# A graph kernel whose final normalization moves from VectorE to ScalarE, with another plan for its banks

## The chip, the core and the metric

The kernel runs on one core of a Trainium2 chip. The metric is the time of one execution on the device, in microseconds (us). The engines of the core are named as in the profile: PE is TensorE (PEld its weight loads), DVE is VectorE, ACT is ScalarE, POOL is GpSimd, SP is SyncE, which here only starts transfers. TensorE writes its results to eight banks of PSUM, each of 128 partitions by 512 fp32 values.

## The reference

128 graphs of 64 nodes with 256 features pass through two layers, each with a residual and a normalization without learned factors. The first layer is attention with 8 heads and a mask for each head, the second a graph network with 4 heads and a gate:

```python
def _layernorm(x, axis=-1, eps=1e-05):
    m = jnp.mean(x, axis=axis, keepdims=True)
    v = jnp.var(x, axis=axis, keepdims=True)
    return (x - m) / jnp.sqrt(v + eps)

def layer0(x, masks):                       # q, k, v: x @ W.T + b, split in 8 heads
    scores = where(mask, q @ k.T / sqrt(32), -1e9)
    return softmax(scores) @ v, merged, @ Wo.T + bo

def layer1(h, adj):                         # 4 heads
    Wh = h @ W.T + bW
    A = tanh(where(adj, (Wh @ attn) @ Wh.T, 0))
    ha = concat(relu(A @ Wh)) @ A_w.T
    hf = h @ fc_w.T
    coeff = sigmoid(hf @ g1_w.T + ha @ g2_w.T + gbias)
    return hf * coeff + ha * (1 - coeff)

h   = _layernorm(x + layer0(x, masks))
out = _layernorm(h + layer1(h, adj))
```

The change touches the last line: how the mean, the variance and the quotient of the second normalization are worked out for each group, and where its input lies meanwhile.

## The kernel before

Eight graphs (512 nodes) form a group; there are 16 groups, 0 to 15. The kernel is written as one program for each engine, in a fixed order, and the engines meet at semaphores. All engines walk through 17 **turns**. A turn has an A group and a B group: it does the first layer of group A and the second layer of group B = A - 1, with the instructions of the two interleaved. `whole(eng, turn)` writes them out: turn 0 (A = 0, no B), turn 1 (1, 0), a hardware loop over turns 2 to 14, turn 15 (A = 15, B = 14), and the last turn (no A, B = 15).

Precise products are made of three fp32r matmuls, so most tensors exist as a high part that ScalarE copies out of a bank (`T_out`, `U_high`, `cat_high`, ...) and a low part that VectorE forms from the same bank (`low`).

**Banks.** Each result of TensorE has a name (T0 to T7, score0 to score3, R0, ...) and a bank. The strings `BODY`, `FIRST` and `LAST` near the top list all results of a turn in TensorE's order as `name:bank`. Before TensorE writes a result, `claim` makes it wait until the result that had this bank before has been released: each bank has a semaphore `taken` that its last reader raises (`take`), and one named `full` that TensorE raises (`filled`) and readers wait for (`await_tile`). A bank is thus a ring: what follows what in it comes from the list alone.

**The end of a group.** Behind the gate, VectorE leaves the transposed sum `rT`. TensorE transposes it back (`res_T`) into the banks R0 and R1, two of the group's four blocks p of 256 features in each, as the last thing of turn g + 1 for B = g. ScalarE copies both to `res` in SBUF (`res_out`, 128x512 each), at the end of the same turn, and in the last turn behind T3 for group 14. At the start of the next turn VectorE takes the moments of `res` (`result_moments`: four BN_STATS, four BN_AGGR, giving mean and variance `mv2`), GpSimd adds EPS and takes the power -0.5 (`root_2`, giving `rstd2`), and VectorE normalizes `res` in place, block by block (`result_normalized`), between its first score tile (`shift(A, 0)`) and its second. SP then stores `res` (`store`, 512 KB). For group 15, functions with `half` in their names do this in the last turn, with VectorE reading the banks; they are the same before and after.

**The start of a turn.** TensorE computes T0, then the scores of A, then T1 to T7, hf0 and the adj products (`adj_scores`, which wait for T4 to T7 to be released). ScalarE copies each T tile out and runs an exponential of the softmax (`exps`) behind T1, T3, T5 and T7, as `EXP_AFTER` says. The softmax of a score tile on VectorE is `shift` (add the mask, take the maximum, subtract it: lines L1112, L1115, L1117), on ScalarE the exponential (L861), on VectorE the sum and its reciprocal, on GpSimd the product of both (L1386).

In the profile's rows a bank is just `bank`. The lines that matter: L389, L390 and L394 are the three matmuls of `dense` (all T tiles among others), L516 the scores, L602 adj, L709 the R transposes; L885 `T_out`, L861 `exps`, L949 `res_out`, L875 at_hi of `attention`, L848 the queries' copy; L1176 and L1180 the moments, L1272 `result_normalized`; L1403 and L1405 `root_2`, L1396 a small product of `root_1`; L699 the last turn's transposes, L1243 its rT.

Of the kernel before, what the change touches and what calls it, by code (L numbers as in the profile page):

```python
# [10 lines left out]
ALU = mybir.AluOpType  # L11
# [26 lines left out]
def listed(text):  # L38
# [9 lines left out]
BODY = ("T0:4 score0:0 score1:1 score2:2 score3:3 T1:5 T2:6 T3:7 T4:4 T5:5 T6:6 T7:7 hf0:4 adj0:5 adj1:6 v0:0 v1:1 "  # L48
        "probT0:2 probT1:3 probT2:0 probT3:1 U000:7 U001:4 U010:5 U011:6 U100:2 U101:3 U110:0 U111:1 attn0:7 attn1:4 "
        "hf1:5 cat0:6 cat1:2 cat2:3 cat3:7 y0:0 y1:1 cat4:4 cat5:5 cat6:6 cat7:7 ha0:4 ha1:5 z0:6 z1:7 hT0:2 hT1:3 ")  # L50
# [8 lines left out]
def stage_kernel(nc, x, xT, adjS, adjT, masks, eye, wq, bq, wk, bk, wv, bv, wo, bo,  # L59
                 Wn, attn, AwT, fcn, g1T, g2T, gb, out):  # L60
    ctx = ExitStack()
    with ctx:
# [21 lines left out]
        def sb(name, shape, dt=F32):  # L84
            return at(name, shape, dt, region(size(shape, dt)))
# [57 lines left out]
        rstd1, rstd2, var1, from1 = (sb(n, [P, NP]) for n in ("rstd1", "rstd2", "var1", "from1"))  # L143
# [55 lines left out]
        zeros_ready = sem("zeros_ready")  # L199

# [87 lines left out]
        def _(sp):  # L288
# [65 lines left out]
            def store(g):  # L354
                sp.wait_ge(out_ready, g * NP + NP)
                carried(sp)
                sp.dma_start(out[bass.ds(g, 1)].rearrange("o p t d -> t (o p) d"), res[:]).then_inc(stored, 16)
# [13 lines left out]
            for s in range(2):  # L371

                sp.wait_ge(out_ready, (GROUPS - 1) * NP + 2 * s + 2)
                sp.dma_start(out[GROUPS - 1, 2 * s:2 * s + 2].rearrange("p t d -> t p d"),
                             res[:, 2 * s:2 * s + 2, :]).then_inc(stored, 16)
# [404 lines left out]
        def _(act):  # L780
# [162 lines left out]
            def res_out(g):  # L943
                if later(g):
                    act.wait_ge(stored, g * 16)
                    carried(act)
                for q2 in range(2):
                    bank = await_tile(act, "B", f"R{q2}", g)
                    take(act.activation(res[:, 2 * q2:2 * q2 + 2, :], pairs_of(bank), ACT.Copy), "B", f"R{q2}", g)  # L949

            def turn(A, B, more):
# [39 lines left out]
                for n in range(KC):  # L991
                    T_out(B, n)
                    if A is None and n == 3:
                        res_out(B - 1)
                    if A is not None and n in EXP_AFTER:
                        exps(A, EXP_AFTER.index(n))
                h_fc(B, 0)
# [26 lines left out]
                if more:  # L1024
                    queries(A + 1)
                    keys(A + 1)
                    res_out(B)
# [4 lines left out]
        def _(dve):  # L1032
# [231 lines left out]
            def result_moments(g):  # L1264
                for q2 in range(2):
                    await_taken(dve, "B", f"R{q2}", g)
                moments(g, res, stats2, mv2, stats2_ready, mv2_ready)

            def result_normalized(g):
                dve.wait_ge(rstd2_ready, g + 1)  # L1270
                for p in range(NP):
                    dve.tensor_scalar(res[:, p, :], res[:, p, :], mv2[:, p, 0:1], rstd2[:, p:p + 1], ALU.subtract,  # L1272
                                      ALU.mult).then_inc(out_ready, 1)

            def turn(A, B, more):
# [27 lines left out]
                if later(B):  # L1303
                    result_normalized(B - 1)
# [36 lines left out]
        def _(pool):  # L1341
# [58 lines left out]
            def root_2(g):  # L1400
                pool.wait_ge(mv2_ready, g * NP + NP)
                carried(pool)
                pool.tensor_scalar(rstd2[:], mv2[:, :, 1], EPS, None, ALU.add).then_inc(root2, 1)  # L1403
                pool.wait_ge(root2, g + 1)
                pool.tensor_tensor(rstd2[:], rstd2[:], half[:], ALU.pow).then_inc(rstd2_ready, 1)  # L1405

# [94 lines left out]
```

## Time and profile before

| | |
|---|---|
| median of 3 runs | 1094.99 us (1093.66 to 1097.73) |
| the profiled execution | 1096.53 us, of which the span from first to last instruction is 1094.4 us |
| mean granted clock of TensorE | 0.998 |
| busy: PE, PEld, DVE, ACT, POOL | 1079.4, 905.4, 732.6, 531.4, 284.1 us |
| instructions | 25365 |
| chain of work that ended last | PE 97%, DVE 2%, DMA 1% |

Busy time of an engine is the time in which at least one of its instructions runs. Matmuls are pipelined, and their ends in the trace are modelled, so the start of one and the start of the next say more than its length. In the rows, "idle before" in brackets is the time for which the engine had stood idle and what ended it; a row without brackets followed the one before it at once. A row with x4 stands for four instructions in a row, with their time together.

### The profile page before, as it was taken

Reading aid. Unit: us, or ns where it says so; the run is one execution under the profiler, and the core shown is the slowest. Engines: PE = TensorE matmul, PEld = TensorE weight load, DVE = VectorE, ACT = ScalarE, POOL = GpSimd, SP = SyncE. Lnnn points to the kernel's source line nnn. Section 1 sums busy time; section 2 is a strip of 40 time slices with the busy share of each in tenths; the row PEclk is TensorE's granted clock in tenths of the full one; section 3 lists DMA queues with packets and bytes.
Section 4 is the critical chain, followed back from the end, with each engine's and each line's share of the span. In section 5 each row is a group of like instructions: output and inputs, shape, how many; then the busy total and the mean of one; then the engine's idle time right before and its main releaser. Section 6 shows DMA issues by size and latency. Waiting matters only on the chain.

```text
span 1094.4 us, 25365 instructions
## 1 busy us (share of the span) xinstructions
PE 1079.4 (99%) x10090; PEld 905.4 (83%) x10090; DVE 732.6 (67%) x1379; ACT 531.4 (49%) x947; POOL 284.1 (26%) x249
## 2 busy tenths in 40 slices
PE   8999999999999999999999999999999999999997
PEld 6888788888888888788888888888888888888886
DVE  7785766767677585765757667585775757667545
ACT  5663453635446363563635446363563635536351
POOL 1542231231322213222231312213222232312200
PEclk9999999999999999999999999999999999999999
DMA  7000100100010000100100010000100001010000
GB/s 263 2 25 19 41 24 27 34 20 19 22 40 22 20 19 22 40 22 20 41 19 21 22 40 22 20 19 22 40 22 20 31 13 37 22 41 3 1 20 20
DMA packets 26860, 32.59 MB, mean 30 GB/s; under 512 B 4432, under 2 KB 23376, under 8 KB 26448
## 3 DMA queue, kind: packets, MB, share of 16 engines
q1 hardware_dynamic: 26400, 31.93, 8.7%
q8 instruction: 21, 0.34, 0.1%
q10 hardware_dynamic: 432, 0.26, 0.1%
q14 instruction: 7, 0.06, 0.0%
HBM read 23.80 MB, written 8.39 MB: 29 GB/s over the span
## 4 chain that ended last, share of the span: by engine, by line
PE 97%; DVE 2%; DMA 1%; issue 0%; POOL 0%; ACT 0%; DVEq 0%
PE bank L389 18%; PE bank L390 17%; PE bank L394 17%; PE bank L381 8%; PE bank L383 8%; PE bank L382 8%; PE bank L602 5%; PE bank L625 4%; PE bank L529 2%; PE bank L516 2%; PE bank L547 2%; PE bank L572 1%; PE bank L709 1%; PE bank L429 0%; DMA raw_q<-in_wq 0%
## 5 line engine op out<-in xcount | busy, mean ns | idle before, releaser
L920 ACT ACTIVATE cat_hi<-bank 128x512 fp32r<-128x512 f32 x128 | 76.6, 598 | 128.5 <-PE bank L394 128.5
L885 ACT ACTIVATE T<-bank 128x512 f32<-128x512 f32 x128 | 75.8, 594 | 78.4 <-PE bank L394 78.1
L1034 DVE SCALAR_TENSOR_TENSOR cat_lo<-bank,cat_hi 128x512 fp32r<-128x512 f32 x128 | 86.5, 685 | 40.6 <-ACT cat_hi L920 39.7
L389 PE MATMUL bank<-hT_hi,g_lo 128*128 128x512 f32 x256 | 102.7, 401 | 0.0
L383 PE MATMUL bank<-cat_hi,aw_hi 128*128 128x512 f32 (+1 forms) x272 | 102.4, 377 | 0.0
L382 PE MATMUL bank<-cat_hi,aw_lo 128*128 128x512 f32 (+1 forms) x272 | 102.4, 377 | 0.0
L381 PE MATMUL bank<-cat_lo,aw_hi 128*128 128x512 f32 (+1 forms) x272 | 102.4, 377 | 0.0
L1386 POOL TENSOR_TENSOR probs<-probs,den 128x512 f32<-128x512 f32 x64 | 67.1, 1059 | 131.5 <-DVE den L1125 131.5
L390 PE MATMUL bank<-hT_hi,g_hi 128*128 128x512 f32 x256 | 99.9, 390 | 0.0
L390 PE MATMUL bank<-U_hi,wt_hi 128*128 128x512 f32 x256 | 99.8, 390 | 0.0
L389 PE MATMUL bank<-U_hi,wt_lo 128*128 128x512 f32 x256 | 99.8, 390 | 0.0
L1034 DVE SCALAR_TENSOR_TENSOR haT_lo<-bank,haT_hi 128x512 fp32r<-128x512 f32 (+1 forms) x34 | 22.4, 660 | 113.1 <-ACT haT_hi L925 106.1
L1034 DVE SCALAR_TENSOR_TENSOR U_lo<-bank,U_hi 128x512 fp32r<-128x512 f32 x128 | 78.0, 681 | 12.9 <-ACT U_hi L914 12.9
L1379 POOL TENSOR_TENSOR y<-y,bo_all 128x1024 f32<-128x1024 f32 x16 | 39.1, 2441 | 176.6 <-ACT at_hi L875 176.6
L925 ACT ACTIVATE haT_hi<-bank 128x512 fp32r<-128x512 f32 x30 | 17.9, 598 | 125.8 <-PE bank L383 125.8
L394 PE MATMUL bank<-hT_lo,g_hi 128*128 128x512 f32 x256 | 78.9, 389 | 0.0
L394 PE MATMUL bank<-U_lo,wt_hi 128*128 128x512 f32 x256 | 78.9, 389 | 0.0
L914 ACT ACTIVATE U_hi<-bank 128x512 fp32r<-128x512 f32 x128 | 64.4, 626 | 7.3 <-PE bank L625 7.3
L1369 POOL TENSOR_TENSOR hT<-hT_hi,hT_lo 128x1024 f32<-128x1024 f32 x16 | 38.8, 2422 | 107.7 <-DVE hT_lo L1034 107.7
L861 ACT ACTIVATE probs<-probs 128x512 f32<-128x512 f32 x64 | 40.4, 632 | 38.5 <-DVE probs L1117 38.4
L382 PEld LDWEIGHTS bank<-cat_hi,aw_lo 128*128 128x128 f32 x272 | 51.2, 188 | 9.4
L381 PEld LDWEIGHTS bank<-cat_lo,aw_hi 128*128 128x128 f32 x272 | 51.2, 188 | 9.4
(183 smaller groups left out, 2768.9 us busy)
## 6 DMA issues: line engine op xcount, KB each, us to landing
y<-in_x SPq DMA_DIRECT2D x16, 512.0 KB, 3.4
out<-res SPq DMA_DIRECT2D x15, 512.0 KB, 3.0
x_raw<-in_xT SPq DMA_DIRECT2D x14, 512.0 KB, 3.3
W_nat<-in_Wn SPq DMA_DIRECT2D x1, 1028.0 KB, 7.7
attn_nat<-in_attn SPq DMA_DIRECT2D x1, 1024.0 KB, 9.9
adjS_u<-in_adjS SPq DMA_DIRECT2D x32, 32.0 KB, 2.7
raw_A<-in_AwT SPq DMA_DIRECT2D x1, 1024.0 KB, 8.7
x_second<-in_xT SPq DMA_DIRECT2D x1, 512.0 KB, 10.1
```

What stands on the lines that cost most here:

```text
L381: pe.matmul(out, asel(a[0]), bsel(b[1]), start=first, stop=False)
L382: pe.matmul(out, asel(a[1]), bsel(b[0]), start=False, stop=False)
L383: return pe.matmul(out, asel(a[0]), bsel(b[0]), start=False, stop=last)
L389: pe.matmul(out, wsel(w[1]), dsel(d[0]), start=first and n == 0, stop=False)
L390: pe.matmul(out, wsel(w[0]), dsel(d[0]), start=False, stop=False)
L394: ins = pe.matmul(out, wsel(w[0]), dsel(d[1]), start=False, stop=last and n == len(terms) - 1)
L602: ins = pe.matmul(bank[b * S:b * S + S, q * D:q * D + D].rearrange("p (h n) -> p h n", h=H2), hT[:, k, first:first + S], T[:, k, :, first: ...
L885: take(act.activation(T[:, n % DC, n // DC, :], bank[:], ACT.Copy), "B", f"T{n}", g)
L914: act.activation(U_hi[:, c, :, first:first + P], bank[:].rearrange("p (h t) -> p h t", h=H2), ACT.Copy).then_inc(U_hi_ready, 1)
L920: act.activation(cat_hi[:, n, :], bank[:], ACT.Relu).then_inc(cat_hi_ready, 1)
L1034: return dve.scalar_tensor_tensor(out=out, in0=bank, scalar=bias, in1=hi.bitcast(F32), op0=op, op1=ALU.subtract)
L1386: pool.tensor_tensor(view, view, den[:, j, :].unsqueeze(2).to_broadcast([P, NG, S]), ALU.mult) \
```

## The change

The change has three parts. First, `res_out` no longer copies: ScalarE writes the normalized result straight from the banks, four activations of 128x256 with the scale `rstd2` and the bias `from2` = -mean x rstd2, one pair for each block. It has moved from the end of the turn to the place behind T1 and the first exponential of the next turn (in the last turn from behind T3 to behind T5), and waits for `from2`. VectorE takes the moments from the banks, and `result_normalized` is gone. Second, GpSimd makes `from2` in two further small instructions. Third, since R0 and R1 now stay in banks 6 and 7 until after T1, `BODY` gives T0 to T3 the banks 4, 5, 4, 5, and banks 4 and 6, and 5 and 7, are exchanged for all results behind. SP's store waits for R0 and R1 to be released instead of for `out_ready`. The `LAST` list is as it was.

```diff
-BODY = ("T0:4 score0:0 score1:1 score2:2 score3:3 T1:5 T2:6 T3:7 T4:4 T5:5 T6:6 T7:7 hf0:4 adj0:5 adj1:6 v0:0 v1:1 "
+BODY = ("T0:4 score0:0 score1:1 score2:2 score3:3 T1:5 T2:4 T3:5 T4:6 T5:7 T6:4 T7:5 hf0:6 adj0:7 adj1:4 v0:0 v1:1 "
...
             def store(g):
-                sp.wait_ge(out_ready, g * NP + NP)
-                carried(sp)
+                for q2 in range(2):
+                    await_taken(sp, "B", f"R{q2}", g)
+                    carried(sp)
                 sp.dma_start(out[bass.ds(g, 1)].rearrange("o p t d -> t (o p) d"), res[:]).then_inc(stored, 16)
...
             def res_out(g):
+
                 if later(g):
                     act.wait_ge(stored, g * 16)
                     carried(act)
-                for q2 in range(2):
-                    bank = await_tile(act, "B", f"R{q2}", g)
-                    take(act.activation(res[:, 2 * q2:2 * q2 + 2, :], pairs_of(bank), ACT.Copy), "B", f"R{q2}", g)
+                act.wait_ge(from2_ready, g + 1)
+                carried(act)
+                for p in range(NP):
+                    bank = bank_of("B", f"R{p // 2}", g)
+                    ins = act.activation(res[:, p, :], bank[:, p % 2 * D:p % 2 * D + D], ACT.Identity,
+                                         bias=from2[:, p:p + 1], scale=rstd2[:, p:p + 1])
+                    if p % 2:
+                        take(ins, "B", f"R{p // 2}", g)
...
                 for n in range(KC):
                     T_out(B, n)
-                    if A is None and n == 3:
-                        res_out(B - 1)
                     if A is not None and n in EXP_AFTER:
                         exps(A, EXP_AFTER.index(n))
+                    if (n == 5 if A is None else n == 1) and later(B):
+                        res_out(B - 1)
...
                 if more:
                     queries(A + 1)
                     keys(A + 1)
-                    res_out(B)
...
             def result_moments(g):
-                for q2 in range(2):
-                    await_taken(dve, "B", f"R{q2}", g)
-                moments(g, res, stats2, mv2, stats2_ready, mv2_ready)
-
-            def result_normalized(g):
-                dve.wait_ge(rstd2_ready, g + 1)
                 for p in range(NP):
-                    dve.tensor_scalar(res[:, p, :], res[:, p, :], mv2[:, p, 0:1], rstd2[:, p:p + 1], ALU.subtract,
-                                      ALU.mult).then_inc(out_ready, 1)
+                    if p % 2 == 0:
+                        bank = await_tile(dve, "B", f"R{p // 2}", g)
+                    dve.bn_stats(stats2[:, p, :], bank[:, p % 2 * D:p % 2 * D + D]).then_inc(stats2_ready, 1)
+                dve.wait_ge(stats2_ready, g * NP + NP)
+                carried(dve)
+                for p in range(NP):
+                    dve.bn_aggr(mv2[:, p, :], stats2[:, p, :]).then_inc(mv2_ready, 1)
...
                 if A is not None:
                     shift(A, 0)
-                if later(B):
-                    result_normalized(B - 1)
...
                 pool.tensor_tensor(rstd2[:], rstd2[:], half[:], ALU.pow).then_inc(rstd2_ready, 1)
+                pool.tensor_scalar(from2[:], mv2[:, :, 0], -1.0, None, ALU.mult).then_inc(neg2, 1)
+                pool.wait_ge(rstd2_ready, g + 1)
+                pool.wait_ge(neg2, g + 1)
+                carried(pool)
+                pool.tensor_tensor(from2[:], from2[:], rstd2[:], ALU.mult).then_inc(from2_ready, 1)
```

The next rows are ScalarE's order at the start of the looped turn, before the change, with what each instruction waits for (`full4` is bank 4 filled, `shifted` a score tile shifted):

```order
L885 ACTIVATE T<-bank 128x512 [waits full4]
L244 REGISTER_ALU
L885 ACTIVATE T<-bank 128x512 [waits full5]
L860 ISA
L861 ACTIVATE probs<-probs 128x512 [waits shifted]
L244 ISA
L885 ACTIVATE T<-bank 128x512 [waits full6]
```

And after it:

```order
L887 ACTIVATE T<-bank 128x512 [waits full4]
L245 REGISTER_ALU
L887 ACTIVATE T<-bank 128x512 [waits full5]
L862 ISA
L863 ACTIVATE probs<-probs 128x512 [waits shifted]
L948 ISA
L954 ACTIVATE res<-bank,from_118,rstd_115 128x256 [waits stored,from2_ready]
L954 ACTIVATE res<-bank,from_118,rstd_115 128x256 x3
L887 ACTIVATE T<-bank 128x512 [waits full4]
```

Four res activations stand between the first exponential and T2, and T2 comes out of bank 4 instead of 6.

TensorE's order before, from the first matmul of T3 to that of T4 (each T tile is six matmuls; the claim of its bank is the wait in front of the first, and L236 only computes what count to wait for):

```order
L389 MATMUL bank<-hT_hi,g_lo 128x512 [waits taken7]
L390 MATMUL bank<-hT_hi,g_hi 128x512
L389 MATMUL bank<-hT_hi,g_lo 128x512
L390 MATMUL bank<-hT_hi,g_hi 128x512
L394 MATMUL bank<-hT_lo,g_hi 128x512 x2
L389 MATMUL bank<-hT_hi,g_lo 128x512 [waits taken4]
```

And after it, the same place:

```order
L391 MATMUL bank<-hT_hi,g_lo 128x512 [waits taken5]
L392 MATMUL bank<-hT_hi,g_hi 128x512
L391 MATMUL bank<-hT_hi,g_lo 128x512
L392 MATMUL bank<-hT_hi,g_hi 128x512
L396 MATMUL bank<-hT_lo,g_hi 128x512 x2
L237 ISA
L391 MATMUL bank<-hT_hi,g_lo 128x512 [waits taken6]
```

The matmuls are the same. T3 now waits for T1's bank, and T4 for bank 6, which R0 had.

## Rows read from the trace of the kernel before

**Rows 1.** the profile's page: the span, then busy time of TensorE (PE)

```profile
span 1094.4 us, 25365 instructions
...
PE 1079.4 (99%) x10090; PEld 905.4 (83%) x10090; DVE 732.6 (67%) x1379; ACT 531.4 (49%) x947; POOL 284.1 (26%) x249
```

**Rows 2.** TensorE's waits, first and last of seven: us in total, times, longest

```profile
PE bank L516 <- issue: 1.8, 2, 1.1
PE bank L699 <- DVE rT L1243: 1.7, 2, 1.4
...
PE bank L475 <- DVE x_lo L1053: 0.2, 1, 0.2
```

**Rows 3.** busy time by stretch (instructions), then granted clock, DMA share, GB/s

```profile
117.00:121.00 4.00, 2.89 (x134) 2.26 (x133) 2.40 (x9) 0.60 (x1) 1.27 (x2) 1.00 0.02 4
512.07:527.11 15.04, 15.04 (x193) 12.28 (x193) 12.46 (x28) 8.06 (x14) 3.35 (x4) 1.00 0.10 35
```

**Rows 4.** TensorE's weight loads (PEld) that begin T3, T4, T5 and T6

```profile
518.57 0.19 PEld L389 LDWEIGHTS bank<-hT_hi,g_lo 128*128 128x128 f32 x1
...
519.93 0.19 PEld L389 LDWEIGHTS bank<-hT_hi,g_lo 128*128 128x128 f32 x1
...
521.29 0.19 PEld L389 LDWEIGHTS bank<-hT_hi,g_lo 128*128 128x128 f32 x1
...
522.65 0.19 PEld L389 LDWEIGHTS bank<-hT_hi,g_lo 128*128 128x128 f32 x1
```

**Rows 5.** ScalarE (ACT) in time order: start us, us, what, idle before

```profile
512.85 1.08 ACT L949 ACTIVATE res<-bank 128x512 f32<-128x512 f32 x2
...
517.62 0.60 ACT L885 ACTIVATE T<-bank 128x512 f32<-128x512 f32 x1 [2.51 <-PE bank L394]
518.16 0.63 ACT L861 ACTIVATE probs<-probs 128x512 f32<-128x512 f32 x1
518.99 0.60 ACT L885 ACTIVATE T<-bank 128x512 f32<-128x512 f32 x1 [0.20 <-PE bank L394]
...
521.50 0.63 ACT L861 ACTIVATE probs<-probs 128x512 f32<-128x512 f32 x1 [0.56 <-DVE probs L1117]
522.04 0.58 ACT L885 ACTIVATE T<-bank 128x512 f32<-128x512 f32 x1
...
540.31 1.63 ACT L875 ACTIVATE at_hi<-bank,bias_v 128x256 fp32r<-128x256 f32 x4
```

**Rows 6.** VectorE (DVE) in time order, the same turn

```profile
514.03 1.41 DVE L1176 BATCH_NORM_STATS2 stats<-res 128x6 f32<-128x256 f32 x4 [3.20 <-ACT res L949]
515.60 0.38 DVE L1180 BATCH_NORM_AGGREGATE mv<-stats 128x2 f32<-128x6 f32 x4 [0.16 <-DVE stats L1176]
515.99 0.69 DVE L1112 TENSOR_TENSOR probs<-bank,mask_static 128x512 f32<-128x512 f32 x1
...
517.43 0.69 DVE L1117 TENSOR_TENSOR probs<-probs,mx 128x512 f32<-128x512 f32 x1
518.04 1.38 DVE L1272 TENSOR_SCALAR res<-res,mv,rstd 128x256 f32<-128x256 f32 x4
```

**Rows 7.** GpSimd (POOL) in time order, the same turn

```profile
488.50 0.20 POOL L1396 TENSOR_TENSOR var<-var,rstd 128x4 f32<-128x4 f32 x1
...
516.17 0.23 POOL L1403 TENSOR_SCALAR rstd<-mv 128x4 f32<-128x4 f32 x1 [7.95 <-DVE mv L1180]
516.48 1.04 POOL L1405 TENSOR_TENSOR rstd<-rstd,half 128x4 f32<-128x4 f32 x1
```

**Rows 8.** ScalarE by line: duration ns min/median/max, first and last start

```profile
L848 ACT ACTIVATE qT<-bank,bias_q x32: 687/690/695, 8.5 to 971.1; 128x512 f32<-128x512 f32 x32
...
L875 ACT ACTIVATE at_hi<-bank,bias_v x64: 467/551/568, 32.6 to 1003.8; 128x256 fp32r<-128x256 f32 x64
```

**Rows 9.** ScalarE and TensorE late in the T tiles of the last turn

```profile
1044.36 0.60 ACT L885 ACTIVATE T<-bank 128x512 f32<-128x512 f32 x1 [0.76 <-PE bank L394]
...
1048.33 0.63 PEld L602 LDWEIGHTS bank<-T,hT 128*64 128x64 f32 x8 [0.35 <-issue]
```

More of the change, by code:

```diff
@@ L47 @@
                "G7:2 W0:5 W1:6 W2:7 W3:1 q0:4 q1:2 FC:5 FF:6 hT0:0 hT1:3 k0:7 k1:1")
-BODY = ("T0:4 score0:0 score1:1 score2:2 score3:3 T1:5 T2:6 T3:7 T4:4 T5:5 T6:6 T7:7 hf0:4 adj0:5 adj1:6 v0:0 v1:1 "
-        "probT0:2 probT1:3 probT2:0 probT3:1 U000:7 U001:4 U010:5 U011:6 U100:2 U101:3 U110:0 U111:1 attn0:7 attn1:4 "
-        "hf1:5 cat0:6 cat1:2 cat2:3 cat3:7 y0:0 y1:1 cat4:4 cat5:5 cat6:6 cat7:7 ha0:4 ha1:5 z0:6 z1:7 hT0:2 hT1:3 ")
+BODY = ("T0:4 score0:0 score1:1 score2:2 score3:3 T1:5 T2:4 T3:5 T4:6 T5:7 T6:4 T7:5 hf0:6 adj0:7 adj1:4 v0:0 v1:1 "
+        "probT0:2 probT1:3 probT2:0 probT3:1 U000:5 U001:6 U010:7 U011:4 U100:2 U101:3 U110:0 U111:1 attn0:5 attn1:6 "
+        "hf1:7 cat0:4 cat1:2 cat2:3 cat3:5 y0:0 y1:1 cat4:6 cat5:7 cat6:4 cat7:5 ha0:6 ha1:7 z0:4 z1:5 hT0:2 hT1:3 ")
 TURN = listed(BODY + "q0:0 q1:1 k0:2 k1:3 R0:6 R1:7")
@@ L142, in stage_kernel @@
         mv1, mv2 = (sb(n, [P, NP, 2]) for n in ("mv1", "mv2"))
-        rstd1, rstd2, var1, from1 = (sb(n, [P, NP]) for n in ("rstd1", "rstd2", "var1", "from1"))
+        rstd1, rstd2, var1, from1, from2 = (sb(n, [P, NP]) for n in ("rstd1", "rstd2", "var1", "from1", "from2"))
         W_nat = at("W_nat", [P, DC * H2, D + 1], F32, r_cat)
@@ L199, in stage_kernel @@
         zeros_ready = sem("zeros_ready")
+        neg2, from2_ready = sem("neg2"), sem("from2_ready")
         def carried(eng):
@@ L371, in _ @@
             for s in range(2):
-                sp.wait_ge(out_ready, (GROUPS - 1) * NP + 2 * s + 2)
+                sp.wait_ge(out_ready, 2 * s + 2)
                 sp.dma_start(out[GROUPS - 1, 2 * s:2 * s + 2].rearrange("p t d -> t p d"),
```

## The prediction

> **What bounds the kernel now.** I began with the page: TensorE is busy 1079.4 of 1094.4 us [rows 1]. Busy time alone proves little for a pipelined engine, so the view of TensorE's waits came next. It has seven lines, which add up to 7.9 us over the whole kernel; the first, second and last stand in [rows 2]: 1.8 us of "issue" in two places, 1.7 us at the very end on VectorE's rT, and 0.2 us. None of the seven occurs more than twice, so none belongs to the repeated turn. The windows view says the same of the part that the diff touches: from the R transposes at 512.07 to the adj products at 527.11 TensorE is busy 15.04 of 15.04 us at granted clock 1.00 (the upper level, 2.4 GHz) [rows 3]. There, the weight loads that begin T3, T4, T5 and T6 come every 1.36 us: 518.57, 519.93, 521.29, 522.65 [rows 4]. TensorE's stream of matmuls is the kernel's length. A change can shorten it only by removing work or a wait from TensorE, and this one removes neither in the loop; it can lengthen it by making one of these loads wait. All else below is about whether one does.
>
> **What is taken away.** ScalarE's two res copies, 1.08 us behind kT at 512.85 [rows 5], and VectorE's four res TENSOR_SCALARs, 1.38 us between the first and second score tile [rows 6]. ScalarE next works on T0, which TensorE paces anyway; VectorE's second shift starts where L1272 stood, at 518.04 [rows 6], 1.3 us sooner, and the softmax chain behind it with it. TensorE waits for neither in the loop, so both savings are worth 0.
>
> **What is added, step by step, in the turn of the rows.**
> 1. Moments. The first res copy starts at 512.85, two take 1.08 [rows 5], the second therefore at about 513.4, so R1 is full by then. The four BN_STATS take 1.41 us [rows 6]; with R0's two run before 513.4 and R1's two after, the last ends at about 514.2. No row here has BN_STATS on a bank in this turn; if it were half as slow again, the end would be 514.6. Then 0.16 + 0.38 for the BN_AGGRs [rows 6]: 514.7. The first shift started at 515.99 directly behind them; now it starts at 516.0 because the score tiles are only then full. Nothing gained, nothing lost.
> 2. GpSimd. It started 0.19 us after the last BN_AGGR (515.98 to 516.17), then 0.23, a gap of 0.08, and 1.04 for the power [rows 7]. From 514.9 that is 516.3. Added are a TENSOR_SCALAR like the 0.23 one and a TENSOR_TENSOR like L1396's 0.20, with two gaps of 0.1: from2 is ready at about 516.9. At worst each costs 1.04 as the power does: 518.6.
> 3. ScalarE comes to the wait for from2 when the first exponential has been issued. That one starts at 518.16, and behind an exponential the next starts 0.54 later (521.50 to 522.04) [rows 5]: 518.70. from2 is there 1.8 us before, and 0.1 before even at its worst. The wait itself costs 0.
> 4. Four res activations, 128x256, with bias and scale both read from a tile. No row shows two such operands. With one, four at_hi ran in 1.63 us [rows 5], each 0.55 [rows 8], so one follows another after 0.36. One bias operand makes 0.69 of 0.60 at 128x512 (L848 [rows 8] against L885 [rows 5]), 0.09 each. My value, nearest to these: 0.64 each, one every 0.45. Lower bound: as at_hi, 0.55 and 0.36. Upper bound: as a whole 128x512 with bias, 0.69 and 0.60.
> 5. R0's bank is given back when the second res ends: 518.70 + 0.45 + 0.64 = 519.79. VectorE began 0.10 after ScalarE's copy ended (513.93 to 514.03) [rows 5, 6]; with that for TensorE it is 519.89, against T4's weight load at 519.93: hidden, by 0.04. Lower bound 519.71. Upper bound 518.70 + 0.60 + 0.69 + 0.10 = 520.09, a wait of 0.16 in each of the 14 turns that have a res_out and a T4 behind it (turns 2 to 15): 2.2 us.
> 6. R1's bank: fourth res ends at 518.70 + 3 x 0.45 + 0.64 = 520.69, with 0.10 520.79, against T5 at 521.29. T2 out then starts at 520.50 instead of 518.99 and ends at 521.10; T6 wants its bank at 522.65. T3 out ends near 521.6, wanted by T7 1.36 later still. The second exponential starts at about 521.5, where it stood before [rows 5], and from there ScalarE is where it was.
> 7. The bank plan. T3 now takes T1's bank: T1 out ends at 518.22 [rows 5], with 0.10 518.32, against 518.57 [rows 4]: hidden by 0.25. T2 takes T0's, given back before T1 begins. Behind T3 the plan is the old one with 4 and 6, and 5 and 7, exchanged. Cost 0.
> 8. The store leaves when R1 is given back, near 520.8, where it left after the last TENSOR_SCALAR (519.4) before; what waits for it are the copies of the U tiles, which stand just ahead of the at_hi copies of 540.31 [rows 5]. Cost 0.
> 9. Last turn, where res_out stands behind T5. T5 out starts at 1044.36 [rows 9]; the R tiles were full two T tiles earlier, at 1044.36 - 0.1 - 2 x 1.36 = 1041.5, and steps 1 and 2 take 3.5 us from there (513.4 to 516.9): from2 at 1045.0, when ScalarE is free (1044.36 + 0.54). Four res, 4 x 0.45, put T6 out at 1046.9 and T7 out at 1047.4 to 1048.0, with 0.10 1048.1, against adj's first load at 1048.33 [rows 9]. Hidden; at the upper bound of step 4, 0.60 each, late by 0.4 us, once.
>
> Sum: 0 us of 1094.4, with 0 to 2.2 us as the bound above. The profiled execution took 1096.53 us, its span 1094.4; the median of the runs is 1094.99, so I forecast 1095.0.
>
> A page names a price for step 4: by the Trainium skill, "ScalarE: Activation LUTs", section "What ACT_TABLE_LOAD costs", each per-partition pointer operand adds about 93 ns to an ACTIVATE with immediates, and neighbours overlap by 93 ns. As an estimate from that page a 128x256 activation with two would last 0.585 us and follow every 0.49; the second res would end at 519.78, T4 would still be met, and the sum stays 0. The 0.09 of the rows agrees; the two-operand case no row here shows.
>
> **Rivals.**
> - *T4 waits for R0 after all, and decides.* Speaking for it: step 5 has 0.04 us to spare, and every later wait would add, since TensorE has no idle time to absorb it. Against: half a percent, 5.5 us over 14 turns, is 0.39 a turn, so the second res would have to end past 520.2, 0.43 later than I reckon, which is more than any row of a 128x256 or 128x512 activation gives. At 1.0 us for each res, say by overhead of two operand reads, the wait is 518.70 + 2.0 + 0.10 - 519.93 = 0.87 a turn, 12 us: 1107. Chance 0.06.
> - *TensorE gains a little.* The two "issue" pauses of 1.8 us in all [rows 2] lie at the scores of the turns that enter and leave the loop; if the code shifted so that they went, 1093.2. For: they are the only idle time near the change. Against: TensorE's instructions do not change. Chance 0.06; over half a percent below, which no wait in the trace could pay for, 0.02.
> - *The clock falls.* Short waits at each bank could cost more than their length if the granted clock fell with them. In the turn that enters the loop TensorE was idle 1.11 of 4.00 us and the granted clock stayed 1.00 [rows 3]. If it fell to the lower level for each T stage, 15.04 us would become 30, 14 times: about 1305. Chance 0.01. The Trainium skill, "TensorE: Matmul & The Clock Gate", section "A second HAM failure mode: psum-queue depth-cycling", warns of just this, short idles from cycling through banks making the clock swing; by that rule two banks under four tiles is the wrong direction, by the row it is harmless.
> - *Forecast*: everything hidden, or a wait up to the bound of step 5. Chance 0.85.
>
> **Numbers.** The likeliest is 1095.0. Its own spread comes from the bound of 2.2 us above, the pauses of 1.8 us below, and the runs themselves, 1093.66 to 1097.73. I give 1092.8 to 1099.0; it leaves out the two large rivals. This kernel's measurement can tell about 0.5% from no change. Faster by more than that 0.02, within it 0.91, slower 0.07.
>
> **What would show it.** After the change: TensorE's waits still near 8 us with no line that occurs 14 times; the T3 to T6 loads still 1.36 us apart; ScalarE's res group as four of 0.5 to 0.7 us starting 0.54 behind the first exponential, with no idle before them; VectorE's second shift 1.3 us sooner; GpSimd's power about 1.3 us sooner. It would be wrong if a line "PEld L391 <- ACT res" appears with 14 times, if ScalarE idles for from2, or if the span grows by more than 2 us.

## The result, and the profile after the change

The changed kernel takes 1093.4 us (1091.98 to 1094.5, 22 runs); the kernel before took 1095.05 (1093.64 to 1097.83, 22 runs) beside it. The ratio is 0.998, interval 0.9974 to 0.9986, so it gained 1.65 us by the medians, and between 1.5 and 2.8 by the interval of the ratio. That is small and inside the range that I gave, but it is more than nothing, and I had said that the change gives TensorE nothing. The cause of this gain is what the rest is about.

The profiled execution's span is 1091.5 us (1094.4 before), at a mean granted clock of 0.998, as before. Busy: TensorE 1078.5, VectorE 708.3 (732.6), ScalarE 541.0 (531.4), GpSimd 291.6 (284.1).

Part of the time line of the changed kernel in the turn of [rows 3 to 7], engine by engine (lines have moved by two: L391 is the old L389, L863 the old L861, L954 the new res activation, L887 `T_out`, L1275 the moments, L1407 and L1414 GpSimd's; L1119 the first step of a shift, old L1112):

```profile
511.32 1.43 DVE L1275 BATCH_NORM_STATS2 stats<-bank 128x6 f32<-128x256 f32 x4 [1.87 <-PE bank L711]
...
516.66 0.68 DVE L1119 TENSOR_TENSOR probs<-bank,mask_static 128x512 f32<-128x512 f32 x1
...
513.47 0.23 POOL L1407 TENSOR_SCALAR rstd<-mv 128x4 f32<-128x4 f32 x1 [6.61 <-DVE mv L1279]
...
515.32 0.20 POOL L1414 TENSOR_TENSOR from<-from,rstd 128x4 f32<-128x4 f32 x1 [0.17 <-issue]
...
516.78 0.64 ACT L863 ACTIVATE probs<-probs 128x512 f32<-128x512 f32 x1
517.32 1.91 ACT L954 ACTIVATE res<-bank,from,rstd 128x256 f32<-128x256 f32 x4
519.12 1.09 ACT L887 ACTIVATE T<-bank 128x512 f32<-128x512 f32 x2
520.07 0.66 ACT L863 ACTIVATE probs<-probs 128x512 f32<-128x512 f32 x1
...
517.19 0.19 PEld L391 LDWEIGHTS bank<-hT_hi,g_lo 128*128 128x128 f32 x1
...
518.55 0.19 PEld L391 LDWEIGHTS bank<-hT_hi,g_lo 128*128 128x128 f32 x1
```

The reader is to see the forecast's steps in it, everything about 1.4 us earlier than before, since this execution is ahead by that much at this turn (0.55 us of it from the first loads, which have nothing to do with the change). The moments are taken from `bank`, not from `res`. GpSimd's last product starts at 515.32 and lasts 0.20: `from2` is there at 515.5, 1.8 us before ScalarE's 517.32 (step 3 said 1.8). ScalarE's four res activations stand 0.54 behind the exponential and end 1.91 us later, without a wait. T2 and T3 follow at 519.12. VectorE's second shift stands at 516.66, and 516.66 + 1.38 is the 518.04 of the forecast. The loads that begin T3 and T4 are 1.36 us apart, and so are those of T5 and T6.

The waits of TensorE in the changed kernel (us in total, times, longest); seven lines before, in all 7.9 us:

```profile
PE bank L701 <- DVE rT L1250: 1.7, 2, 1.4
PE bank L409 <- POOL hf L1346: 1.3, 1, 1.3
PE bank L531 <- POOL probs L1390: 1.1, 2, 0.8
PE bank L518 <- issue: 1.1, 1, 1.1
PE bank L518 <- ACT kT L855: 1.0, 1, 1.0
PE bank L604 <- ACT T L887: 0.4, 1, 0.4
```

No line occurs 14 times. Compared with before, one of the two pauses at the scores (L518, the old L516) is gone, so are two waits in the first loads (0.8 us together), and one line is new: L604, adj, waits 0.4 us for ScalarE, once, in the last turn. By this view the two kernels differ in single waits, and the repeated turn is free of waits in both. That view is where my prediction stopped, and it does not show where the time went. The starts of matmuls do. From the first attention product of turn 2 to that of turn 14 are 12 turns. Before, with VectorE's copies of the low parts of U beside them (L1034):

```profile
143.05 0.36 PE L547 MATMUL bank<-PT,v 64*32 64x64 f32 x18
...
538.31 0.28 PE L625 MATMUL bank<-A_hi,h_hi 64*128 64x256 f32 x2
538.64 0.29 PE L547 MATMUL bank<-PT,v 64*32 64x64 f32 x9
...
537.10 4.87 DVE L1034 SCALAR_TENSOR_TENSOR U_lo<-bank,U_hi 128x512 fp32r<-128x512 f32 x8 [0.84 <-ACT U_hi L914]
...
934.24 0.36 PE L547 MATMUL bank<-PT,v 64*32 64x64 f32 x19
```

And after (attention's product is L549, `U_lo` L1041):

```profile
142.36 0.35 PE L549 MATMUL bank<-PT,v 64*32 64x64 f32 x17
...
536.93 0.28 PE L627 MATMUL bank<-A_hi,h_hi 64*128 64x256 f32 x2
537.16 0.36 PE L549 MATMUL bank<-PT,v 64*32 64x64 f32 x18
...
535.72 4.88 DVE L1041 SCALAR_TENSOR_TENSOR U_lo<-bank,U_hi 128x512 fp32r<-128x512 f32 x8 [0.85 <-ACT U_hi L916]
...
931.96 0.36 PE L549 MATMUL bank<-PT,v 64*32 64x64 f32 x18
```

Before, 934.24 - 143.05 = 791.19, or 65.933 us a turn; after, 931.96 - 142.36 = 789.60, or 65.800. Each looped turn is 0.13 us shorter. The middle rows show where: the last pair of U matmuls starts 0.33 before the first attention product in the kernel before, 0.23 in the changed one. The trace gives each of these matmuls 0.28, although the next pair starts 0.12 behind it; so of the 0.33 most lies under the modelled length of the last pair, and only 0.06 shows as idle time of TensorE. That is too short for the list of waits, but a window over the place has it, 3.94 busy of 4.00 us before and 4.00 of 4.00 after:

```profile
535.00:539.00 4.00, 3.94 (x90) 3.60 (x89) 2.59 (x5) 3.52 (x9) 0.00 (x0) 1.00 0.00 0
```

```profile
535.00:539.00 4.00, 4.00 (x168) 3.73 (x165) 3.28 (x6) 3.91 (x9) 0.00 (x0) 1.00 0.00 0
```

Before, such a gap of 0.06 stands at the attention products of every looped turn, and TensorE has no other idle time from turn 2's products to turn 14's; after, it has none at all there. The queue of weight loads has more of it; its waits for this line, before and then after:

```profile
PEld bank L547 <- issue: 3.9, 16, 0.3
```

```profile
PEld bank L549 <- issue: 0.9, 3, 0.3
```

Sixteen times before, three times after: the loop's thirteen are gone, and the three left are turns outside of it.

What TensorE waits for there is in the code of `attention`. It claims the banks of attn0 and attn1, which U000 and U001 had, and waits until the softmax's banks (`probT`) and those of v have been released. VectorE releases U001's bank last. One `U_lo` lasts 0.69 and eight take 4.87, so one follows another after 0.60, and the second ends at 537.10 + 0.60 + 0.69 = 538.39 before and at 537.01 after: attention's product starts 0.25 behind it before, 0.15 after. So both kernels wait for the same release, and differ in how long TensorE takes to start behind it. The order of the built programs offers the reason, which the experiments test. Before, in the loop:

```
L625 MATMUL bank<-A_hi,h_hi 128x4x64 x2
L547 MATMUL bank<-PT,v 32x64 [waits taken7,taken1,taken4,taken0,taken2,taken3]
```

After, in the loop:

```
L627 MATMUL bank<-A_hi,h_hi 128x4x64 x2
L237 REGISTER_ALU [waits taken0,taken1,taken3,taken2]
L237 REGISTER_ALU [waits taken5]
L549 MATMUL bank<-PT,v 32x64 [waits taken6]
```

The late one is taken4 before (U001 is in bank 4) and taken6 after (banks 4 and 6 were exchanged). Before, TensorE's queue has one more instruction with waits, that for taken2 and taken3, behind the one that holds taken4; after, taken6 stands last and nothing is behind it. (The first row of waits in the list above stands for several instructions; five in all wait in the loop after the change, three before.) The source asks for both in the same order; the builder of the program lays the waits out differently once the bank list differs. In turns 1 and 15, outside of the loop, the layout is the old one in both kernels.

The last turn goes the other way. The moments, the last step of `from2`, ScalarE from T5's copy on and the weight loads there, after the change:

```profile
1037.85 1.43 DVE L1275 BATCH_NORM_STATS2 stats<-bank 128x6 f32<-128x256 f32 x4 [1.97 <-PE bank L711]
...
1041.85 0.20 POOL L1414 TENSOR_TENSOR from<-from,rstd 128x4 f32<-128x4 f32 x1 [0.17 <-issue]
...
1041.02 0.60 ACT L887 ACTIVATE T<-bank 128x512 f32<-128x512 f32 x1 [0.76 <-PE bank L396]
1042.17 1.93 ACT L954 ACTIVATE res<-bank,from,rstd 128x256 f32<-128x256 f32 x4 [0.55 <-POOL from L1414]
1043.99 1.09 ACT L887 ACTIVATE T<-bank 128x512 f32<-128x512 f32 x2
...
1044.22 0.41 PEld L396 LDWEIGHTS bank<-hT_lo,ff_hi 128*128 128x128 f32 x2
1045.41 0.66 PEld L604 LDWEIGHTS bank<-T,hT 128*64 128x64 f32 x8 [0.77 <-issue]
```

ScalarE idles 0.55 us for `from2`, the four res take 1.93, T6 and T7 are out at 1045.08, and adj's first load comes at 1045.41, 0.77 us after the loads of hf end; before it was 0.35 [rows 9]. That costs 0.42 to 0.45 us, once.

The sum by the trace: 13 looped turns at 0.13 give 1.7, and the last turn loses 0.45; together 1.3 us gained, against 1.65 by the medians and 1.5 to 2.8 by the interval. (The gap of turn 15 before and that of turn 1 after are 0.43 here, and 0.34 in other executions of the same turns, in c0 and e3 below; they are left out of the sum, in which they would cancel.) The profiled executions differ by more, 2.9, because 0.96 lies in a pause at the scores of turn 15 that this execution lacks, and 0.55 in the first loads, before any work of the change.

### The profile page after: what moved, and what is told of

The parts are those of the page before. It is cut to its first block and busy times, and to the rows that moved or that the text cites. A ratio compares the mean times of both kernels' runs of the same rounds, so it can differ in the third digit from the quotient of the medians.

```text
span 1091.5 us, 25383 instructions
## 1 busy us (share of the span) xinstructions
PE 1078.5 (99%) x10090; PEld 906.0 (83%) x10090; DVE 708.3 (65%) x1319; ACT 541.0 (50%) x977; POOL 291.6 (27%) x279
## 5 line engine op out<-in xcount | busy, mean ns | idle before, releaser
L887 ACT ACTIVATE T<-bank 128x512 f32<-128x512 f32 x128 | 75.1, 604 | 87.0 <-PE bank L396 87.0
L1041 DVE SCALAR_TENSOR_TENSOR cat_lo<-bank,cat_hi 128x512 fp32r<-128x512 f32 x128 | 86.6, 687 | 39.1 <-ACT cat_hi L922 37.0
L391 PE MATMUL bank<-hT_hi,g_lo 128*128 128x512 f32 x256 | 102.7, 401 | 0.0
L391 PE MATMUL bank<-U_hi,wt_lo 128*128 128x512 f32 x256 | 99.7, 389 | 0.0
L1041 DVE SCALAR_TENSOR_TENSOR haT_lo<-bank,haT_hi 128x512 fp32r<-128x512 f32 (+1 forms) x34 | 22.5, 660 | 113.0 <-ACT haT_hi L927 106.0
L1041 DVE SCALAR_TENSOR_TENSOR U_lo<-bank,U_hi 128x512 fp32r<-128x512 f32 x128 | 78.0, 684 | 12.9 <-ACT U_hi L916 12.9
L604 PE MATMUL bank<-T,hT 128*64 128x256 f32 x512 | 58.8, 382 | 0.4 <-ACT T L887 0.4
```

The costliest lines, as they stand in the source:

```text
L391: pe.matmul(out, wsel(w[1]), dsel(d[0]), start=first and n == 0, stop=False)
L604: ins = pe.matmul(bank[b * S:b * S + S, q * D:q * D + D].rearrange("p (h n) -> p h n", h=H2), hT[:, k, first:first + S], T[:, k, :, first: ...
L887: take(act.activation(T[:, n % DC, n // DC, :], bank[:], ACT.Copy), "B", f"T{n}", g)
L1041: return dve.scalar_tensor_tensor(out=out, in0=bank, scalar=bias, in1=hi.bitcast(F32), op0=op, op1=ALU.subtract)
```

## The experiments

Theory A: the gain comes from the bank list alone, by the number of instructions that TensorE's queue still has to pass behind the wait that is released last. Rival B: it comes from the pauses at the scores, [rows 2]. Rival C: it comes from the moved res work (VectorE's and ScalarE's relief). A second question was what the bank plan is for, which I had priced at nothing, and a third how much room step 5 has.

**c0_before_again**: the kernel before, unchanged.

> The kernel before, unchanged, profiled once more, to see which of its pauses come back. In the first profile the attention products began 0.33 us after the last pair of U matmuls in every looped turn, and TensorE paused 0.72 us within the scores of the turn behind the loop. Both theories expect the 0.33 us again. If the pause behind the loop belongs to the program (its position among the fetched instructions) it comes back with 0.7 us, if it is chance it does not.

It took 1093.57 us (one run), span 1091.4. Its TensorE waits, in part:

```profile
engine line waited for: us in total, times, longest us
PE bank L699 <- DVE rT L1243: 1.7, 2, 1.4
...
PE bank L516 <- ACT kT L853: 1.0, 1, 1.0
```

There is no line "L516 <- issue": the pauses of [rows 2], 1.8 us, are absent from this execution of the same program, while the gap ahead of the attention products is 0.33 to 0.34 in every turn, and the turn 65.925. Two other kernels that were profiled twice say the same: x1 has such a pause, 1.3 us, and its repetition x4 none; b1 has one, 0.8 us, and b2 none. So the pauses come and go from one execution to the next, while the turn's length is a property of the kernel. B explains the 0.96 above, and it cannot explain 0.13 in each of the looped turns. How often the pauses come in either kernel was not counted, so a part in the ratio is not ruled out.

**p2_plan_only**: before, with the new list and nothing else.

```diff
-BODY = ("T0:4 ... T1:5 T2:6 T3:7 T4:4 T5:5 T6:6 T7:7 hf0:4 ...
+BODY = ("T0:4 ... T1:5 T2:4 T3:5 T4:6 T5:7 T6:4 T7:5 hf0:6 ...
```

> Before, with the new bank list for the looped body and nothing else: res is still copied and normalized as before. My theory: the gain in the loop comes from the bank list alone, because with it the waits in front of the attention products are laid out anew, and the wait that ends last (for the bank of U001, which VectorE gives back) stands last instead of in the middle. It expects the attention products 0.23 us behind the last U pair instead of 0.33, 0.10 us less in each of the 13 looped turns, 1.3 us less in all. The rival (the work taken from ScalarE's turn end and from VectorE's softmax stretch frees something that TensorE waited for) expects 0.33 us and no change, since that work is back.

1093.31 us (1092.21 to 1096.52, 12 runs), ratio 0.999, interval 0.9979 to 1.0001: the time alone does not separate it from no change. The trace does: turn 65.795, gap 0.22 to 0.23 in the loop and 0.34 in turns 1 and 15, and the weight loads' line falls from 16 times to 3, as in the changed kernel (the span is 1089.9 against c0's 1091.4, neither with a pause at the scores):

```profile
PEld bank L547 <- issue: 0.8, 3, 0.3
```

The built program has the waits in the order of the changed kernel. The list alone shortens the turn; the res work has no part in it.

**x1_attn1_last**: before, old list, with the late wait put last by hand.

```diff
 def attention(...):
-    for b in range(2):
-        claim(pe, "A", f"attn{b}", g)
-    carried(pe)
+    claim(pe, "A", "attn0", g)
+    carried(pe)
+    claim(pe, "A", "attn1", g)
+    carried(pe)
```

> Before, with the old bank list, but the wait for U001's bank written as the last thing in front of the attention products, behind a semaphore increment, so that one wait instruction follows where the late one stood second of three. My theory expects 0.21 to 0.25 us from the last U pair to the attention products instead of 0.33, in the looped turns and in the one behind the loop, about 1.3 to 1.4 us less than before. The rival expects 0.33 us and no change.

1092.84 us (1091.87 to 1094.12, 12 runs), ratio 0.9983, interval 0.9974 to 0.9992: faster by 2.1 us at the medians, with no part of the change in it; 15 turns at 0.13 account for 2.0. The built program ends these waits with taken4 (`[waits taken1,taken7,taken0,taken2,taken3,taken4]`), and the trace has the short gap in all turns, 1 and 15 too:

```profile
535.74 0.28 PE L626 MATMUL bank<-A_hi,h_hi 64*128 64x256 f32 x2
535.97 0.76 PE L548 MATMUL bank<-PT,v 64*32 64x64 f32 x55
```

That is 0.23, and the turn is 65.801, as short as the changed kernel's.

**x2_attn1_first**: the changed kernel, with attn1 claimed ahead of the waits for probT.

```diff
+    claim(pe, "A", "attn1", g)
+    carried(pe)
...
-    for b in range(2):
-        claim(pe, "A", f"attn{b}", g)
+    claim(pe, "A", "attn0", g)
     carried(pe)
```

> The changed kernel, with the wait for U001's bank written first, so that four more wait or register instructions follow it in the loop before the attention products can begin. My theory expects the gap to grow from 0.23 us to 0.4 to 0.6 us, by 2 to 5 us over the looped turns: 1095.5 to 1098 us. The rival (what matters is when ScalarE and VectorE are done, not the order in which TensorE asks) expects 0.23 us and 1093.4 us.

1098.97 us (1098.79 to 1102.92, 6 runs), ratio 1.0045, interval 1.0029 to 1.0061. Now four instructions stand behind the late wait in the loop and three in turns 1 and 15. The gap is 0.69 in the loop, long enough that TensorE's own waits show it, and 0.60 in turns 1 and 15:

```profile
538.88 0.28 PE L628 MATMUL bank<-A_hi,h_hi 64*128 64x256 f32 x2
539.57 0.66 PE L550 MATMUL bank<-PT,v 64*32 64x64 f32 x43 [0.41 <-issue]
```

```profile
PE bank L550 <- issue: 6.1, 15, 0.4
```

The release comes from the same `U_lo`; only the queue behind it is longer. The turn is 66.283, 0.48 above the changed kernel's. I had expected 0.4 to 0.6 and at most 1098 us: the way was right, the size too low.

**x3_two_behind**: x1 with two more `carried(pe)` behind the late wait, so two plain instructions of the queue that wait for nothing late.

```diff
     claim(pe, "A", "attn1", g)
     carried(pe)
+    carried(pe)
+    carried(pe)
```

> The kernel before with the late wait moved last, as in x1_attn1_last, and then two more semaphore increments on TensorE's queue between that wait and the attention products. They do nothing that anyone waits for. If each sequencer instruction behind the late wait costs about 0.12 us (from 0.33 us with one behind, 0.69 with four), the gap is 0.23 + about 0.2 = 0.43 to 0.48 us in turns 1 to 15, the turn 0.2 to 0.25 us longer than in x1_attn1_last: about 1096 us. If it were register arithmetic and waits on registers that cost, and not the number of instructions, 0.23 us.

1097.31 us (1096.52 to 1101.4, 8 runs), ratio 1.0021, interval 1.0011 to 1.0031. The gap is 0.53 in turns 1 to 15, the turn 66.118. I had expected 0.43 to 0.48, so the direction held and the size was too low: two cost 0.30, not 0.2.

**x4_attn1_last_again**: x1 once more, beside b2 below.

> x1_attn1_last once more, on the same chip as the next one. By the traces both have turns of 65.80 us, 0.23 us at attention and no wait at adj in the last turn, so the theory expects equal times, near 1092.5 us. In separate jobs they were 1092.84 and 1091.79 us.

1092.01 us (1091.65 to 1093.34, 7 runs), ratio 0.9973, interval 0.9962 to 0.9984; turn 65.795, gap 0.22 to 0.23. x1's gain is there again, 3.1 us at the medians this time, of which 15 turns at 0.13 account for 2.0; the interval, 1.8 to 4.2 us, holds both.

Gaps by what stands behind the late wait: nothing 0.23, one 0.33, two plain ones 0.53, three 0.60, four 0.69. The number of all such instructions does not order them: three before (0.33), five in the changed kernel (0.23), four in x1 (0.23). Theory A holds. One thing is not parted for the single step from 0.23 to 0.33: in the kernel before, the late wait also shares its instruction with that for taken0. In x2 and x3 it stands alone, and what is behind it costs 0.12 to 0.15 each.

**e3_last_turn_T7**: the changed kernel with `res_out` behind T7 in the last turn.

```diff
-                    if (n == 5 if A is None else n == 1) and later(B):
+                    if (n == 7 if A is None else n == 1) and later(B):
```

> The changed kernel with res_out of the last turn behind T7 instead of T5, everything else the same. Only the last turn can change. In the changed kernel T7 was copied out 0.33 us before adj's first weight load, which came 0.45 us later than before. My theory: four res activations (1.9 us) ahead of T6 and T7 cost this 0.45 us; with them behind T7 it is gone, adj's first load follows hf0 after 0.46 us as before, and TensorE's line of 0.4 us for T disappears: 1093.0 us. The rival (the 0.45 us come from the bank names or the shifted code) expects it to stay.

1093.43 us (1092.55 to 1097.53, 11 runs), ratio 0.9987, interval 0.9977 to 0.9997. The weight loads ahead of adj:

```profile
1044.30 0.41 PEld L396 LDWEIGHTS bank<-hT_lo,ff_hi 128*128 128x128 f32 x2
1045.07 1.06 PEld L604 LDWEIGHTS bank<-T,hT 128*64 128x64 f32 x12 [0.35 <-issue]
```

Idle 0.35 again, as in [rows 9], and TensorE's L604 line is gone: the 0.4 us was the position behind T5. The median shows nothing of it (1093.4 for the changed kernel, measured at another time); 0.4 us is below what these runs resolve.

**p1_res_only**: the changed kernel with the old list.

```diff
-BODY = ("T0:4 ... T1:5 T2:4 T3:5 T4:6 T5:7 T6:4 T7:5 hf0:6 ...
+BODY = ("T0:4 ... T1:5 T2:6 T3:7 T4:4 T5:5 T6:6 T7:7 hf0:4 ...
```

> The other half of the change alone: res_out behind the first exponential, moments from the banks, but with the old bank list, in which T2 and T3 take banks 6 and 7 that R0 and R1 still hold. T2's weight load stands at 4.6 us behind T0's start and R0 is given back 2.4 us later, so my theory expects TensorE to wait some 2.4 to 2.7 us for T2 in each of 14 turns, about 35 us in all: 1127 to 1131 us, and 0.33 us from U to attention, as in the kernel before. If R0's release were not what T2 waits for, the time would stay near 1093 to 1095 us.

1131.27 us (1129.75 to 1136.25, 4 runs), ratio 1.0334, interval 1.0307 to 1.0361. With T2 in R0's bank, TensorE waits for the res activations in every turn, and the turn has 2.46 us more in 12 of 14. The gap ahead of the attention products is 0.34 in every turn, as in the kernel before, although the res work has moved; that speaks against rival C once more:

```profile
PE bank L391 <- ACT res L954: 30.5, 14, 2.2
```

In two turns, the first of the loop and one in its middle, it was 4.1, and in both the granted clock fell. Windows of busy time in the second of them (TensorE first, the granted clock third from the end):

```profile
465.00:466.00 1.00, 0.00 (x0) 0.00 (x0) 0.96 (x2) 1.00 (x3) 0.00 (x0) 1.00 0.00 0
...
469.00:470.00 1.00, 1.00 (x4) 0.71 (x4) 0.56 (x1) 0.00 (x0) 0.00 (x0) 0.50 0.93 310
...
471.00:472.00 1.00, 1.00 (x6) 0.82 (x5) 0.20 (x1) 0.77 (x2) 0.00 (x0) 0.93 0.00 0
```

TensorE was idle for 2.2 us, as in every other turn, and the clock then stood at the lower level, 0.50 of full speed, for three microseconds; at 122 to 127 it did so too. Behind the same waits of the other 12 turns it stayed at 1.00. So my rival "the clock falls" has something in it, behind two of 14 such idle stretches, at 1.6 us each (4.1 less 2.5), and the changed kernel has no such stretch in its T tiles. The plan is what makes the rest of the change possible: without it the change costs 36 us.

**e4_res_after_T2**: the changed kernel with `res_out` one T tile later.

```diff
-                    if (n == 5 if A is None else n == 1) and later(B):
+                    if (n == 5 if A is None else n == 2) and later(B):
```

> The changed kernel with res_out one place later in the looped turn, behind T2 instead of behind the first exponential. ScalarE then starts it 0.83 us later or more (T2 is full 0.8 us behind the first exponential's start, its copy takes 0.54), so R0 is given back about 1.4 us later than now, where the margin before T4's weight load was some 0.2 us. My accounting expects T4 to be late by 0.6 to 0.7 us in each of 14 turns, 8.4 to 10 us: 1101.8 to 1103.4 us. If TensorE had slack that takes up such a wait, less.

1100.67 us (1099.45 to 1101.27, 4 runs), ratio 1.0046, interval 1.003 to 1.0061. ScalarE's res, the loads that begin T3 and T4:

```profile
520.47 1.93 ACT L954 ACTIVATE res<-bank,from,rstd 128x256 f32<-128x256 f32 x4
...
519.55 0.19 PEld L391 LDWEIGHTS bank<-hT_hi,g_lo 128*128 128x128 f32 x1
...
521.53 0.19 PEld L391 LDWEIGHTS bank<-hT_hi,g_lo 128*128 128x128 f32 x1 [0.66 <-ACT res L954]
```

T4's load would stand at 519.55 + 1.36 = 520.91. R0 is given back when the second res ends, 520.47 + 0.45 + 0.56 = 521.48, and the load follows 0.05 later. T4 is late by 0.62, as expected. The turn is 0.565 longer, 14 times 7.9 us, and the time 7.3 over the changed kernel, less than the 8.4 to 10 that I had expected; where the turn wins back the difference was not traced. Here nothing stands behind the late wait that costs a tenth: the claim is carried by the load itself.

**b1_both_mended**: the changed kernel with x1's edit and e3's.

> The changed kernel with both flaws mended: res_out of the last turn behind T7, and the wait for U001's bank last in front of the attention products in every turn. My theory expects 0.23 us from U to attention in all of turns 1 to 15 (0.2 to 0.3 us less than the changed kernel over turns 1 and 15), 0.45 us less in the last turn: 1092.7 us, no better than the kernel before with the one wait moved (1092.84). If moving the res work off ScalarE and VectorE were worth anything of itself, this one would be below 1092.

1091.79 us (1091.37 to 1092.76, 5 runs), ratio 0.9966, interval 0.9952 to 0.998; gap 0.22 to 0.23 in all turns, adj 0.45 sooner. It is below both kernels, and below the 1092 that I had named as the sign that the res work is worth something after all. As five runs are few and the time was lower than the trace accounts for, it was run again.

**b2_both_mended_again**: the same kernel, beside x4.

> b1_both_mended once more beside x4_attn1_last_again. Equal to it within 0.5 us if moving the res work is worth nothing; 1 us below it if the res work was worth something that the traces do not show.

1092.01 us (1091.57 to 1095.87, 12 runs), ratio 0.9972, interval 0.9959 to 0.9986. x4, which has none of the change but the order of the two claims, has the same median, and the turns are 65.795 and 65.800. With the waits in the same order, the res work on ScalarE instead of VectorE is worth nothing in the traced turn and nothing that these runs resolve (their intervals reach 1.2 to 1.5 us to either side), and rival C falls.

## Why the prediction was wrong where it was

**The step that failed is 7**, "The bank plan… Cost 0", and with it the opening claim that the change removes no wait from TensorE in the loop. I had worked out for each T tile whether its bank is back in time, which was right, and took that as all a bank plan can do. It also sets which waits stand together ahead of the attention products, and which of them is last. The term that I put at 0 measured -0.13 us a turn, 13 times, 0.10 of it at the gap. p2 shows that the list alone does it, x1 that the old list does it too when the late wait is last, x2 and x3 that instructions behind the late wait bring it back and more.

That the time still lies in the range is owed to the room that I left for the pauses and the spread of the runs, not to the mechanism.

**The opening reading** failed because I took "busy 15.04 of 15.04" and a list of waits without a repeated line as proof that TensorE never idles in the loop. The window ended at 527.11, and the attention products stand at 538.64, so it did not hold the place; the list leaves out waits as short as 0.06. The window 535 to 539 would have shown 3.94 of 4.00. Even that is only 0.06 of the 0.10, since the rest lies beneath the modelled ends of the short matmuls. The starts have all of it, and the waits view of the weight loads, which I didn't read, repeats it 16 times.

**Steps 1 to 3** held: `from2` 1.8 us ahead of ScalarE in the loop; in the last turn ScalarE does idle for it, 0.55 us.

**Step 4** had 0.64 for each res; the median is 0.56, one every 0.45 as taken. By "ScalarE: Activation LUTs", section "What ACT_TABLE_LOAD costs", in the Trainium skill my estimate was 0.585 and 0.49: nearer in length, farther in spacing. **Step 5**, R0 back 0.04 before T4 wants it, was tighter than the truth: 517.32 + 0.45 + 0.56 = 518.33 against 518.55, 0.22 apart. ScalarE starts 1.23 ahead of T4's load in both, forecast and trace; the difference is the 0.08 of step 4, and the 0.10 that I had allowed from release to load, which e4 shows as 0.05: 0.17 to spare. **Steps 6 and 8** held.

**Step 9** gave hidden, or 0.4 us late, once, at the upper bound. It was late by 0.42 to 0.45, but not for the bound's reason: the four res took 1.93, not 2.4. Two terms were mis-sized. `from2` came later than I had it: T5 out starts at 1041.02 and res at 1042.17, 1.15 behind it, where the forecast had 0.64 (1044.36 to 1045.0). From the first BN_STATS to the end of `from2` it is 4.2 us in the last turn (1037.85 to 1042.05) and in the loop (511.32 to 515.52); I had counted 3.5, from too late a start. ScalarE idled 0.55 for it, one of the signs of being wrong that the forecast names. So T7 was out at 1045.08, later by 0.4 than my latest. The second term is the 0.10 from a release to the next start: the load came 0.33 behind T7. In the built program the wait for T7's bank stands first there, with two more instructions behind it, where e4's is carried by the load itself and costs 0.05. That fits theory A, but the order was not changed at this place, so it is not shown here.

**The rivals.** "TensorE gains a little" had 0.06 and gave the pauses as its reason: the time came near its 1093.2, its mechanism did not. The pauses come and go, as c0 shows, and the gain in the turn is not theirs. "T4 waits" did not happen; e4 made it happen, with T4 late by the 0.62 that the arithmetic of step 5 gives for its later start, and p1 did the same to T2. "The clock falls" did not happen in the changed kernel; it did in p1, behind two idle stretches of 14.

**What stays open.** Besides the 0.10 at the gap each turn is 0.03 shorter in small steps that I can't place; x1, whose turn is 65.801 with the old list and the old res work, has them too, so they come with the order of the waits. Turns at 0.13 and the last turn's loss make 1.3 us, a little below the interval's 1.5 and 0.35 short of the 1.65 at the medians; that rest has no cause shown. Why the builder lays the waits out as it does was not tried; the built programs show only that it changes with the list. The pauses at the scores have no cause shown.

## What to carry to other kernels

Before saying that TensorE never waits, measure from start to start at each place where it claims banks, and read the waits of the weight loads; a busy share of 100% over short matmuls proves nothing to a tenth of a microsecond, and nothing at all about a place outside its window. Where several waits stand in front of one instruction, put the one that is released last at the end: here it was worth 0.10 us a turn at the place and 2 to 3 us of 1095 in all (x1 and x4; the traces account for 2.0). And when a plan of banks or buffers changes, compare the order of waits in the built program, not only which buffer comes free when.

## What the runs showed of the hardware

Each instruction of TensorE's queue that stands behind a late wait delays the next start by 0.10 to 0.15 us, even when it has nothing left to wait for: gaps of 0.23, 0.33, 0.53, 0.60 and 0.69 us for none, one, two, three and four. The step from none to one was measured with the late wait sharing its instruction with another. A wait carried by the load itself lets it start 0.05 us after the release (e4). Pauses of 0.7 to 1.3 us at the scores of the turns that enter and leave the loop are there in some executions of a program and not in others (before and c0, x1 and x4, b1 and b2). After idle stretches of up to 2.2 us the granted clock stayed 1.00 in 12 of 14 turns; in two it was 0.50 for some three microseconds (p1); in x3's profiled execution it fell to 0.50 once, for as long, at a pause of 2.4 us early in the kernel.
